# The first batch of a Mamba and expert layer: four transfers on each of two queues, and a wait for each block of u

## The chip, the cores and the metric

The kernel runs as one program on one core of a Trainium2 chip. The metric is the device time of one execution in microseconds (us); less is better. The core has a matrix engine (TensorE, PE in the rows; its weight loads are PEld), three engines for elementwise work (VectorE or DVE, ScalarE or ACT, GpSimd or POOL), and SyncE (SP), which here only issues DMA transfers. Each engine works through its own instructions in the order in which they are written, and waits on semaphores for the others.

## What is computed

Eight sequences of 512 tokens with 512 channels, all in float32. Each goes through a Mamba block, a residual with layer norm, a mixture of 8 experts (2 per token), and a second residual with layer norm. Cut to what matters here:

```python
xz = einsum('bld,ed->bel', hidden_states, in_proj_w)      # 512 -> 2 x 1024 channels
x, z = xz[:, :1024], xz[:, 1024:]
x = silu(causal_conv(x, conv_w, 4 taps) + conv_b)         # "u" in the kernel
x_dbl = einsum('bdl,kd->blk', x, x_proj_w)                # the x-projection: 1024 -> 64
dt_lo, B, C = x_dbl[..., :32], x_dbl[..., 32:48], x_dbl[..., 48:]
delta = softplus(dt_lo @ dt_proj_w.T + dt_proj_b)
h = h * exp(delta * A) + delta * B * x                    # 512 steps in time, 16 states
y = (sum(h * C) + x * D) * silu(z)
x1 = layernorm(hidden + y @ out_proj_w.T)
out = layernorm(x1 + top2_experts(x1))
```

## The kernel before, in words

The 1024 inner channels lie in 8 blocks of 128 partitions, the 512 tokens along the free dimension. The kernel is a pipeline over the batches. For each batch the three elementwise engines and TensorE run 128 rows (16 states by 8 channel blocks): ACT makes `dA` = exp(delta * A), POOL makes `dbu` = u * B, DVE runs the scan into `hst`, TensorE turns the result and DVE adds it into `y`. Between these rows a planner places, ahead of time, the pieces of the neighbouring batches: the projections of the next, the output and the experts of the one before. Its result is a fixed order of instructions on each engine.

The first batch has nothing to overlap with. Its pieces form a segment of their own, `SEG_FIRST`, which is run before any scan:

- `x`, j = 0..7: four matmuls (k = 0..3, named "shares") of `hT` (the batch's input, turned, four blocks of 128 x 512) with `W` (a 512-wide half of the input weights, `("Wx", 0)` in `delta[0][:, 0:4]` for j below 4, `("Wx", 1)` for the others) into one of two PSUM banks. In the trace each float32 matmul is two records, so one piece is 8 records. ACT then takes the first tap of the convolution (line 1247), DVE the other three (line 1528), and these free the bank.
- `sig`, `sig2`: the SiLU of each block, three ACT instructions and one product on POOL (line 1424), which raises `x_ready` by one for each block of `u`.
- `xproj`: eight shares, each a matmul of one block of `u` with `w_x`, summed in one bank (line 1035); ACT copies the sum to `xdbl`. Behind it stand `Ct` (line 1123) and, in turns, `yinit` (transposes of u * D, line 1067, copied by DVE) and `dt` (line 1129) with softplus on ACT (lines 1292 to 1299).
- POOL forms u = delta * u (line 1453) for each block, and then the first `dbu` (line 1465) and the first scan (line 1671) follow.

The loads of the head are issued by SP in the order written: `hT`, `("Wx", 0)`, the convolution's `cw` and `cb`, `("Wx", 1)`, `w_x`, nine small constants, the weights of z. `hidT_in` and `w_loaded[2]` tell PE that the first two have landed. The x-projection waits like this, and its waits stand ahead of its first share alone:

```python
if w.seg is SEG_FIRST:
    pe.wait_ge(const_in, 16 * NCONST)
    pe.wait_ge(pads_ready, 3)
pe.wait_ge(wx_in, w.p * 16 + 16)
pe.wait_ge(x_ready, w.p * ND + ND)
```

## Time and profile before

| | |
|---|---|
| median of 3 runs | 2383.67 us |
| lowest, highest | 2380.72, 2389.34 us |
| the profiled execution's own time | 2397.16 us |
| its span | 2395.4 us |
| PE busy | 2132.5 us (89% of the span) |
| DVE busy | 2120.6 us (89%) |
| POOL busy | 1804.7 us (75%) |
| ACT busy | 1517.4 us (63%) |
| span up to the first scan (DVE line 1671) | 84.1 us |

The first three lines are device times without the profiler. The others are of one profiled execution; its time is its span and 1.8 us around it. Busy shares are averages over the whole span: what one stretch waits for is read from its own rows.

### The profile page before, as it was taken

Reading aid. Unit: us, or ns where it says so; the run is one execution under the profiler, and the core shown is the slowest. Engines: PE = TensorE matmul, PEld = TensorE weight load, DVE = VectorE, ACT = ScalarE, POOL = GpSimd, SP = SyncE. Lnnn points to the kernel's source line nnn. Section 1 sums busy time; section 2 is a strip of 40 time slices with the busy share of each in tenths; the row PEclk is TensorE's granted clock in tenths of the full one; section 3 lists DMA queues with packets and bytes.
Section 4 is the critical chain, followed back from the end, with each engine's and each line's share of the span. In section 5 each row is a group of like instructions: output and inputs, shape, how many; then the busy total and the mean of one; then the engine's idle time right before and its main releaser. Section 6 shows DMA issues by size and latency. Waiting matters only on the chain. (4 is left out here: it accounts for less than half of the span.)

```text
span 2395.4 us, 30145 instructions
## 1 busy us (share of the span) xinstructions
PE 2132.5 (89%) x8604; PEld 1227.1 (51%) x8604; DVE 2120.6 (89%) x2440; ACT 1517.4 (63%) x2678; POOL 1804.7 (75%) x1448
## 2 busy tenths in 40 slices
PE   7886879898989989899899998899898998879998
PEld 2444555555545555545555555455555454555543
DVE  3799999999999899989999899998999898899933
ACT  3747755776577665668566675777657685565411
POOL 1759997788887888869887798878888697786502
PEclk9898789889998999989998899989999899879999
DMA  3312031347544584446752476445744467575523
GB/s 99 145 49 88 19 123 62 105 162 244 181 118 141 177 277 127 120 146 209 259 126 93 150 249 230 114 141 180 273 123 124 140 209 251 117 246 175 183 85 83
DMA packets 203683, 367.93 MB, mean 154 GB/s; under 512 B 28376, under 2 KB 32600, under 8 KB 203520
## 3 DMA queue, kind: packets, MB, share of 16 engines
q1 hardware_dynamic: 190976, 336.65, 42.3%
q0 software_dynamic: 12544, 29.37, 5.8%
q8 instruction: 71, 1.16, 0.2%
q14 instruction: 92, 0.75, 0.1%
HBM read 287.05 MB, written 78.91 MB: 153 GB/s over the span
## 5 line engine op out<-in xcount | busy, mean ns | idle before, releaser
L1465 POOL TENSOR_TENSOR dbu<-u,Bbc 128x512 f32<-128x512 f32 x896 | 1146.2, 1314 | 243.1 <-DVE hst L1671 234.9
L1671 DVE TENSOR_TENSOR_SCAN hst<-dA,dbu 128x512 f32<-128x512 f32 x896 | 1052.7, 1208 | 19.3 <-ACT dA L1370 15.0
L1370 ACT ACTIVATE dA<-delta,negA 128x512 f32<-128x512 f32 (+1 forms) x1152 | 724.4, 639 | 482.5 <-DVE hst L1671 388.8
L1049 PE MATMUL hTp<-ident,hst 128*128 128x128 f32 x4096 | 584.0, 295 | 126.6 <-DVE hst L1671 35.8
L1049 PEld LDWEIGHTS hTp<-ident,hst 128*128 128x128 f32 x4096 | 508.1, 152 | 363.5 <-issue 142.3
L1497 DVE SCALAR_TENSOR_TENSOR y<-hTp,Ct,y 128x1024 f32<-128x1024 f32 x512 | 647.4, 1265 | 46.6 <-PE hTp L1049 46.0
L1035 PE MATMUL bank<-wslot,hidT 128*128 128x512 f32 x512 | 238.9, 600 | 17.8 <-ACT zs L1314 13.8
L1035 PE MATMUL bank<-delta,tokT 128*128 128x512 f32 x480 | 224.4, 604 | 1.5 <-issue 0.8
L1035 PE MATMUL bank<-wslot,tokT 128*128 128x512 f32 x464 | 221.8, 608 | 2.7 <-ACT tokT L1329 1.7
L1473 POOL TENSOR_TENSOR dbu<-u,Bbc 128x512 f32<-128x512 f32 x128 | 163.3, 1311 | 80.0 <-DVE hst L1679 72.8
L1035 PE MATMUL bank<-hidT,wslot 128*128 128x512 f32 x384 | 193.6, 649 | 12.4 <-DVE u L1528 9.7
L1528 DVE SCALAR_TENSOR_TENSOR u<-bank,cw,u 128x511 f32<-128x511 f32 (+2 forms) x192 | 142.4, 744 | 35.9 <-ACT u L1247 31.1
L1035 PEld LDWEIGHTS bank<-wslot,hidT 128*128 128x128 f32 x512 | 91.9, 192 | 108.5 <-issue 85.8
L1418 POOL DMA_INDIRECT ysb<-sorted_results,place x52 | 81.4, 1566 | 85.9 <-DMA ysb<-x_scratch 76.6
L1035 PEld LDWEIGHTS bank<-wslot,tokT 128*128 128x128 f32 x464 | 83.3, 194 | 89.4 <-issue 80.0
L1035 PEld LDWEIGHTS bank<-delta,tokT 128*128 128x128 f32 x480 | 87.1, 195 | 81.3 <-issue 79.7
L1035 PEld LDWEIGHTS bank<-hidT,wslot 128*128 128x128 f32 x384 | 75.5, 209 | 101.7 <-issue 75.9
L1424 POOL TENSOR_TENSOR u<-u,side 128x512 f32<-128x512 f32 x64 | 81.6, 1275 | 57.0 <-ACT side L1265 56.8
L1453 POOL TENSOR_TENSOR u<-delta,u 128x512 f32<-128x512 f32 x64 | 81.9, 1280 | 28.9 <-DVE delta L1545 23.5
L1083 PE MATMUL hTp<-ident,zs 128*128 128x128 f32 x420 | 69.1, 309 | 29.2 <-DMA zs<-sorted_tokens 19.0
L1432 POOL TENSOR_TENSOR zs<-zs,side 128x512 f32<-128x512 f32 x64 | 87.7, 1370 | 9.9 <-ACT side L1321 9.9
L1247 ACT ACTIVATE u<-bank,cb,cw 128x512 f32<-128x512 f32 x64 | 49.5, 773 | 70.3 <-PE bank L1035 70.0
(149 smaller groups left out, 2558.9 us busy)
## 6 DMA issues: line engine op xcount, KB each, us to landing
wslot<-in_w_expT SPq DMA_DIRECT2D x85, 1024.0 KB, 6.3
Bbc<-b_scratch SPq DMA_DIRECT2D x113, 256.0 KB
zs<-sorted_tokens SPq DMA_DIRECT2D x105, 256.0 KB, 3.2
sorted_results<-ysb SPq DMA_DIRECT2D x105, 256.0 KB, 6.0
wslot<-in_w_inT SPq DMA_DIRECT2D x26, 1024.0 KB, 5.4
res<-in_w_expT SPq DMA_DIRECT2D x18, 1024.0 KB, 6.0
gate_scratch<-zs SPq DMA_DIRECT2D x64, 256.0 KB, 2.0
delta<-in_w_outT SPq DMA_DIRECT2D x14, 1024.0 KB, 9.8
```

What stands on the lines that cost most here:

```text
L1035: mm = nc.tensor.matmul(dst, lhs(k), rhs(k), start=(k == 0), stop=(k == n - 1))
L1049: mm = nc.tensor.transpose(hTp[q % 2][:, tok(j)], hst[n % 2][:, j, start:start + P], ident[:, :])
L1370: nc.scalar.activation(decay_of(step, halved), delta[w.odd][:, j, cols], ACT.Exp, scale=negA[:, j, n:n + 1]).then_inc(exp_done, 1)
L1418: nc.gpsimd.indirect_dma_start(rows_of(w, t), None, ys_dram[:, :], bass.IndirectOffsetOnAxis(ap=place[:, w.odd, t, c:c + 1], axis=0), comp ...
L1424: nc.gpsimd.tensor_tensor(x_j, x_j, side[j % 2][:, :], ALU.mult).then_inc(x_ready, 1)
L1432: nc.gpsimd.tensor_tensor(zs[i % 2][:, :], zs[i % 2][:, :], side[i % 2][:, :], ALU.mult).then_inc(z_ready, 1)
L1453: nc.gpsimd.tensor_tensor(x_j, d, x_j, ALU.mult).then_inc(u_ready, 1)
L1465: nc.gpsimd.tensor_tensor(dbu[j % 4][:, :], u[w.odd][:, j, :], Bbc[n % 2][:, :], ALU.mult).then_inc(dbu_done, 1)
L1473: nc.gpsimd.tensor_tensor(dbu[k % 4][:, :].rearrange("p (k t) -> p k t", k=2), u[w.odd][:, j:j + 2, cols], Bbc[n % 2][:, cols].unsqueeze(1 ...
L1497: nc.vector.scalar_tensor_tensor(y_part, hTp[q % 2][:, :], Ct[odd][:, t, n:n + 1], y_part, ALU.mult, ALU.add).then_inc(acc_done, 1)
L1528: tap = nc.vector.scalar_tensor_tensor(late, bank[s][:, 0:L - k], cw[:, j, TAPS - 1 - k:TAPS - k], late, ALU.mult, ALU.add)
L1671: nc.vector.tensor_tensor_scan(hst[n % 2][:, j, :], dA[j % 2][:, :], dbu[j % 4][:, :], 0.0, ALU.mult, ALU.add).then_inc(scan_done, 1)
```

## The change

The input `hT` of the first batch comes in four transfers, one for each block of 128 rows, each with a semaphore (`head_in`). Its first weights come in four transfers too, one for each 128 columns, that is for each of the pieces x 0 to x 3, each with a semaphore (`head_w`); they are issued by ACT ahead of its table load, on ACT's queue. A row of such a weight transfer has 128 floats (512 bytes) where it had 512 (2 KB). SP raises the two semaphores of before (`hidT_in`, `w_loaded[2]`) by hand, so that the counts of all later batches stay. The x-projection of the first batch waits for `x_ready` at each of its eight shares, for as many blocks of `u` as that share needs, and no more for all eight at its start.

```diff
@@ semaphores
+        head_in = [sem(f"head_in{k}") for k in range(KD)]
+        head_w = [sem(f"head_w{j}") for j in range(KD)]
@@ sync
-            sync.dma_start(hT[:, :, :], hidT[0].rearrange("(k p) t -> p k t", p=P)).then_inc(hidT_in, 16)
-            sync.dma_start(delta[0][:, 0:KD, :], block_src(("Wx", 0))).then_inc(w_loaded[2], 16)
+            for k in range(KD):
+                sync.dma_start(hT[:, k, :], hidT[0, k * P:(k + 1) * P, :]).then_inc(head_in[k], 16)
+            sync.sem_inc(hidT_in, 16)
+            sync.sem_inc(w_loaded[2], 16)
@@ tensor, piece "x"
                     if j == 0 and share == 0:
                         pe.wait_ge(hidT_in, w.p * 16 + 16)
+                    if w.seg is SEG_FIRST and share == 0 and j < KD:
+                        pe.wait_ge(head_w[j], 16)
+                    if w.seg is SEG_FIRST and j == 0:
+                        pe.wait_ge(head_in[share], 16)
@@ tensor, piece "xproj"
                         pe.wait_ge(wx_in, w.p * 16 + 16)
-                        pe.wait_ge(x_ready, w.p * ND + ND)
+                        if w.seg is not SEG_FIRST:
+                            pe.wait_ge(x_ready, w.p * ND + ND)
+                    if w.seg is SEG_FIRST:
+                        pe.wait_ge(x_ready, share + 1)
@@ scalar
+            for j in range(KD):
+                act.dma_start(delta[0][:, 0:KD, tok(j)], block_src(("Wx", 0))[:, :, tok(j)]).then_inc(head_w[j], 16)
             nc.scalar.preload_act_table_set("natural_log_exp_and_others")
```

On PE, at the start of the program and at the x-projection, the order before reads (a row is a line, an operation, output<-inputs and the waits in front of it; the last two rows of the first part are the x-projection and the transposes of `yinit`):

```order
L1035 MATMUL bank0<-hidT,delta0 128x512 [waits hidT_in,w_loaded2]
L1035 MATMUL bank0<-hidT,delta0 128x512 x3
L1035 MATMUL bank1<-hidT,delta0 128x512 [waits w_loaded2]
...
L1035 MATMUL bank0<-u0,spare0 64x512 [waits wx_in,pads_ready,x_ready,const_in,bank_taken0]
L1035 MATMUL bank0<-u0,spare0 64x512 x7
L1067 MATMUL hTp0<-ident,side0 128x128 [waits xd_ready]
```

and with the change:

```order
L1039 MATMUL bank0<-hidT,delta0 128x512 [waits head_w0,head_in0,hidT_in,w_loaded2]
L1039 MATMUL bank0<-hidT,delta0 128x512 [waits head_in1]
L1039 MATMUL bank0<-hidT,delta0 128x512 [waits head_in2]
L1039 MATMUL bank0<-hidT,delta0 128x512 [waits head_in3]
L1039 MATMUL bank1<-hidT,delta0 128x512 [waits head_w1,w_loaded2]
...
L1039 MATMUL bank0<-u0,spare0 64x512 [waits wx_in,pads_ready,x_ready,const_in,bank_taken0]
L1039 MATMUL bank0<-u0,spare0 64x512 [waits x_ready] x7
L1071 MATMUL hTp0<-ident,side0 128x128 [waits xd_ready]
```

No instruction of PE has moved: waits were added, and one wait is now spread over eight matmuls. At the start of ACT the order with the change is

```order
L1222 DMA delta<-in_w_inT 128x4x128 x4
L1223 ACT_TABLE_LOAD
L1260 ACTIVATE u<-bank,cb,cw 128x512 [waits bank_full0,conv_in]
```

so four issues of a DMA stand ahead of the table load, which was ACT's first instruction. On SP one transfer of 1 MB left its place as second, and the first became four.

## Rows read from the trace of the kernel before

**Rows 1.** The page: busy tenths of DVE in 40 equal slices.

```profile
DVE  3799999999999899989999899998999898899933
```

**Rows 2.** Waits of 0 to 60 us: engine, line <- releaser: total, times, longest.

```profile
PE bank L1035 <- DMA delta<-in_w_inT: 9.3, 1, 9.3
...
PE bank L1035 <- POOL u L1424: 7.0, 1, 7.0
```

**Rows 3.** Timeline of the head: start, us, engine, line, operation, [idle before].

```profile
0.75 0.44 SPq L783 DMA_DIRECT2D hidT<-in_hidT  x1
...
2.34 3.08 SPq L787 DMA_DIRECT2D cb<-in_conv_b  x1
5.46 3.22 SPq L788 DMA_DIRECT2D delta<-in_w_inT  x1
...
9.32 31.56 PE L1035 MATMUL bank<-hidT,delta 128*128 128x512 f32 x64 [9.32 <-DMA delta<-in_w_inT]
...
16.07 0.78 ACT L1247 ACTIVATE u<-bank,cb,cw 128x512 f32<-128x512 f32 x1 [14.05 <-PE bank L1035]
```

**Rows 4.** Busy time by stretch; the last three columns are clock, DMA share, GB/s.

```profile
0.00:2.00 2.00, 0.00 (x0) 0.00 (x0) 0.68 (x3) 1.25 (x1) 0.20 (x4) 1.00 0.08 8
2.00:4.00 2.00, 0.00 (x0) 0.00 (x0) 0.00 (x0) 0.03 (x1) 0.00 (x0) 1.00 0.94 216
4.00:5.00 1.00, 0.00 (x0) 0.00 (x0) 0.00 (x0) 0.00 (x0) 0.00 (x0) 1.00 1.06 414
5.00:6.00 1.00, 0.00 (x0) 0.00 (x0) 0.00 (x0) 0.00 (x0) 0.00 (x0) 1.00 1.04 399
6.00:8.00 2.00, 0.00 (x0) 0.00 (x0) 0.00 (x0) 0.00 (x0) 0.00 (x0) 1.00 1.04 395
...
13.00:14.00 1.00, 1.00 (x3) 0.48 (x2) 0.00 (x0) 0.00 (x0) 0.00 (x0) 1.00 1.27 272
...
26.00:28.00 2.00, 2.00 (x6) 0.91 (x5) 0.57 (x2) 1.70 (x3) 1.05 (x1) 1.00 0.00 0
```

**Rows 5.** DMA issues of 0 to 110 us: KB each, us from issue to landing.

```profile
hidT<-in_hidT SPq DMA_DIRECT2D x1, 1024.0 KB, 5.4
...
cb<-in_conv_b SPq DMA_DIRECT2D x1, 4.0 KB, 7.6
```

**Rows 6.** Timeline of TensorE's weight loads in the first piece.

```profile
14.60 0.34 PEld L1035 LDWEIGHTS bank<-hidT,delta 128*128 128x128 f32 x1 [0.52 <-issue]
...
15.81 0.19 PEld L1035 LDWEIGHTS bank<-hidT,delta 128*128 128x128 f32 x1 [0.24 <-issue]
```

**Rows 7.** Timeline of POOL: the last two of its eight products into u.

```profile
43.25 1.26 POOL L1424 TENSOR_TENSOR u<-u,side 128x512 f32<-128x512 f32 x1 [2.47 <-ACT side L1265]
46.47 1.26 POOL L1424 TENSOR_TENSOR u<-u,side 128x512 f32<-128x512 f32 x1 [1.95 <-ACT side L1265]
```

**Rows 8.** Timeline at the x-projection, and ACT's copy of it.

```profile
47.84 0.88 DVE L1536 TENSOR_SCALAR side<-u,dskip 128x512 f32<-128x512 f32 x2 [3.49 <-POOL u L1424]
...
47.88 9.52 PE L1035 MATMUL bank<-u,spare 128*64 128x512 f32 x16 [7.00 <-POOL u L1424]
...
57.43 0.59 ACT L1269 ACTIVATE rows<-bank 64x512 f32<-64x512 f32 x1 [10.84 <-PE bank L1035]
```

**Rows 9.** Busy time by stretch around the x-projection, columns as in rows 4.

```profile
48.00:52.00 4.00, 4.00 (x5) 1.04 (x6) 0.72 (x2) 0.00 (x0) 0.00 (x0) 0.50 0.00 0
...
53.00:56.00 3.00, 3.00 (x9) 0.95 (x8) 0.00 (x0) 0.00 (x0) 0.00 (x0) 1.00 0.00 0
```

**Rows 10.** Timeline from the x-projection to the first scan.

```profile
71.23 0.69 ACT L1292 ACTIVATE zs<-bank,dtb 128x512 f32<-128x512 f32 x1 [1.28 <-PE bank L1129]
...
82.76 9.86 POOL L1465 TENSOR_TENSOR dbu<-u,Bbc 128x512 f32<-128x512 f32 x8
84.13 6.12 DVE L1671 TENSOR_TENSOR_SCAN hst<-dA,dbu 128x512 f32<-128x512 f32 x5 [2.73 <-POOL dbu L1465]
```

**Rows 11.** Busy time by stretch after the first scan, columns as in rows 4.

```profile
84.00:400.00 316.00, 254.10 (x1032) 153.00 (x1031) 306.40 (x285) 214.52 (x354) 276.09 (x224) 0.86 0.21 71
```

## The prediction

> **What bounds the kernel now.** I read the page's slices first. DVE is at 8 or 9 tenths almost from end to end, but shows 3 and 7 in its first two slices of 60 us [rows 1]: there is a head that the pipeline doesn't fill. The stretch behind it does have a bound: from 84 to 400 us DVE is busy 306.4 of 316 us [rows 11]. So a head that is shorter by some us moves everything behind it forward by as much; nothing there waits for a fixed moment, since all its loads are issued in answer to this same work.
>
> In the head I looked at who waits for whom. TensorE has just two long waits in the first 60 us: 9.3 us for the transfer of the first weights, and 7.0 us for POOL's last product into u, ahead of the x-projection [rows 2]. Both lie on the chain to the first scan. From 9.32 us TensorE works through the x pieces with 31.56 us of work without a real gap [rows 3], so whatever starts it earlier moves the end of the x pieces, and POOL's products with them. And while the x-projection runs, ACT sits idle for 10.84 us until its copy at 57.43 [rows 8]. From there to the first `dbu` at 82.76 and the scan at 84.13 it is ACT's softplus that goes on, its longest pause behind the first `dt` 1.28 us [rows 10]. The change touches the two waits, and these alone.
>
> **The x-projection.** Its 16 records start at 47.88, when POOL's last product (46.47 + 1.26 = 47.73) is done, and end at 57.40 [rows 7, 8]. What will be left of it behind 47.88? By then TensorE has been free since 9.32 + 31.56 = 40.88 [rows 3]. The seventh block of u is ready at 43.25 + 1.26 = 44.51, the eighth 3.2 us later [rows 7]; the sixth, one such turn before the seventh, is ready at about 41, and the five before it are earlier. So shares 0 to 5 can run at once from about 41.0: 12 records. A record takes 0.43 us at TensorE's upper clock level (a weight load of 0.19 and 0.24 idle before it, at 15.81) and 0.86 us at the lower one (0.34 and 0.52, at 14.60) [rows 6]. They end at 41.0 + 12 x 0.43 = 46.2, share 6 at 47.0, and share 7 waits for POOL. Its two records start at 47.88 and 48.31, and the last takes some 0.6 us to its end (57.40 less 47.88 is 9.52; six starts 0.86 apart and nine 0.43 apart are 9.0 and leave the last record's own length of some 0.5 to 0.6): 48.9. The x-projection ends 57.4 - 48.9 = **8.5 us** earlier.
>
> This sum has a clock in it. In the trace the granted clock is 0.50 of full (the 1.2 GHz level) in the first 4 us of the x-projection and 1.00 (2.4 GHz) only from 53 us on [rows 9], after TensorE had stood still for 7.0 us [rows 2]. With the change it stands still for under 1 us in that place (47.0 to 47.88), so I take the upper level. Were share 7 alone at the lower level, it would end at 47.88 + 0.86 + 1.1 = 49.8 and the gain be 7.6; with all 16 records there, at 41.0 + 16 x 0.86 + 0.2 = 55.0, a gain of 2.4. [...]
>
> What stands behind: `yinit` needs DVE's two products, which start at 47.84 when the last block of u is there and take 0.88 us [rows 8], so they are ready at 48.7, before TensorE is. ACT has nothing else to do. Both waits that are passed at share 0 (`const_in`, `wx_in`) are for transfers of the head, and by 26 us nothing moves any more [rows 4]. The seven added waits sit on a queue that would idle anyway: nothing.
>
> **The head.** TensorE starts at 9.32 when 2 x 1.05 MB have landed. How fast do they come? From the GB/s of rows 4, times their length: 16 kB by 2 us, 448 kB by 4, 862 kB by 5, 1261 kB by 6, 2051 kB by 8. The 1.05 MB of `hT` are through at 5.5 by this count, and have landed for the semaphore at 0.75 + 5.4 = 6.15 [rows 3, 5], 0.7 us later. With the change the first matmul needs `hT`'s block 0 and the weights of x 0, 262 kB each. Rows of 512 bytes are nowhere near in the head as large transfers; the nearest are the 256-byte rows of `w_x`, at 272 GB/s around 13 us against 395 to 414 for 2 KB rows [rows 4]. So 262 kB of weights cost between 0.66 and 0.96 us; I add the whole 0.3 us.
>
> The unknown is how the 16 DMA engines share between two queues that are full at once; no stretch of the head shows it. Bounds: if they take turns by transfer, 524 kB come first, at 4.2 + 0.3 + 0.7 = 5.2 us. If ACT's queue with its small rows moves only as much as is left, the weights of x 0 come behind all of `hT`, after 1311 kB: 6.1 + 0.3 + 0.7 = 7.1 us. I take two blocks of `hT` ahead of them (786 kB, 4.8 + 0.3 + 0.7): **5.8 us, 3.5 us earlier**, with 4.1 and 2.2 as the bounds. The later blocks hide: x 0 runs at 1.7 us per share on the lower level (0.86 per record), so block 3 is wanted at 5.8 + 5.1 = 10.9 and x 1's weights at 12.6, while all 2.1 MB are through at about 8.2 + 1.2 + 0.7 = 10.1 (four weight transfers at 0.3 more each).
>
> ACT's first tap needs `cw` and `cb`. `cb` landed at 2.34 + 7.6 = 9.9 [rows 3, 5], and now stands behind half as much in its own queue, but shares the engines with rows that are up to 1.2 us slower: 11.1 at the latest. It is wanted when x 0 is done, 5.8 + 6.75 = 12.5 (ACT's tap came at 16.07, 6.75 us after TensorE's start) [rows 3]. The cover is 1.4 us. `("Wx", 1)`, whose issue sat for 3.22 us, is wanted at x 4, beyond 20 us. Four issues on ACT, at 0.44 us each as SP's first or at up to 3.2 each where they stall as SP's fifth did [rows 3], put the table load between 2.5 and 13.5 us, the last of which would just reach the 12.5; a stall at all four at once I don't expect. SP's two `sem_inc` come after four issues, at about 2.8 us: hidden.
>
> **The sum.** 8.5 + 3.5 = 12.0 us. The profiled execution took 2397.16 us and would take 2385.2; it lies 13.5 us above the median of the runs, and I take the same 12.0 off that: 2383.67 - 12.0 = **2371.7 us**, 0.50% less. What a measurement of this kernel can tell from no change is about 0.5%, here 11.9 us, so my forecast lies on that line.
>
> **The rivals.**
>
> *Weights behind all of hT.* TensorE starts at 7.1, the head gives 2.2: 10.7 in all, 2373.0 us. For it: 512-byte rows get little from turns taken row by row. Against: nothing in the trace.
>
> *The head gives nothing.* The first weights come only when all 2.1 MB are through, since the total to be moved is the same; then TensorE starts at 9.3 or later and 8.5 us are left: 2375.2 us. It would need ACT's queue to start after SP's is dry; ACT issues nothing before 0.74 us, as SP does, which speaks against it. The Trainium skill (DMA: Bandwidth & Descriptors, "Rules for kernel authors") speaks against this part of the change: it wants 1 MB and more in a transfer and says that a second issuing engine brings no bandwidth. By that rule the last byte comes no sooner, and this rival is what it gives if the first piece gets no turn of its own.
>
> *The x-projection stays slow.* TensorE's clock is at the lower level in the last shares, or in all: gain 7.6 or 2.4 in place of 8.5, with the head 11.1 or 5.9: 2372.6 to 2377.8 us.
>
> *What is behind the first scan gives or takes.* From 66 us TensorE was at the lower level and held ACT up for 1.28 us at 71.23 [rows 10]; which stretches are slow can fall otherwise. I allow 2 us either way: 2369.7 or 2373.7. A gain that is lost whole, at 2383.7, would need some work tied to the clock on the wall, and I see none.
>
> *Slower.* The waits at every share of x 0 keep TensorE from ever reaching the upper level in the x pieces. They have 64 records; at 0.86 us all take 55.0 in place of 31.56 us, 23.5 more. With 12.0 won that ends 11.5 later, 2395.2 us. It turns into a loss once some 28 more of the 64 records (12.0 / 0.43) run at the lower level than the first 7. The shares are wanted 1.7 us apart and come faster than that, so I give it little.
>
> **How the numbers follow.** Forecast (TensorE starts between 5.2 and 6.6, x-projection at the upper level): 0.52, and a little over a third of it falls short of the line by itself. Weights behind all of `hT`: 0.17. No gain from the head: 0.07. Slow x-projection: 0.08. More than 13 us: 0.08; some taken back behind: 0.05. Slower: 0.03. Faster by over 0.5% are some 0.32 of the forecast's 0.52, the 0.08, and what the scatter of the medians lifts over the line from the next ones, 0.06: 0.46. Slower by over 0.5%: 0.03. The rest, 0.51, is within. The range: the cases without a loss run from 2369.7 to 2377.8, and the three runs shown scatter by 3 to 6 us around their median, so 2365 to 2380.
>
> **What would show it.** In the profile of the changed kernel: TensorE's first matmul between 5.2 and 7.1 us, released by a DMA; records of the first piece at 0.86 us and no gap between its shares; ACT's first tap released by PE and not by `cb`; the x-projection split, most of it before POOL's last product, two records behind it, clock at 1.00; ACT's copy of it within 1.2 us of POOL's last product, where it was 9.7; the first scan near 72 us. It is wrong if the first scan comes at 72 and the end doesn't move with it, or if the first tap waits for its constants.

## The result, and the profile after

The changed kernel takes 2381.79 us (median of 20 runs, 2373.11 to 2388.38), the kernel before in the same measurement 2393.39 us (20 runs, 2377.06 to 2403.39). The ratio is 0.996 with a 95% interval of 0.9941 to 0.9978: by the ratio the change saves about 9.6 us, between 5.3 and 14.1 of 2393. (The two medians differ by 11.6 us, the two means by 9.7.) The forecast was 12.0 us less, a ratio of 0.995, and that is inside. The forecast time, 2371.7 us, and its range up to 2380 are both missed, because of the level that I took the 12.0 off: 2383.67 us from the three runs shown, where twenty say 2393.39.

The profiled execution took 2381.42 us, its span is 2379.6 (before: 2397.16 and 2395.4). The page's tenths of DVE, which answer to [rows 1], have 5 where they had 3 in the first slice; the second still has 7:

```profile
DVE  5799999999999999999999899998999898899833
```

The waits of 0 to 60 us, as in [rows 2]. Both long ones have shrunk, from 9.3 to 5.1 and from 7.0 to 0.8:

```profile
PE bank L1039 <- DMA delta<-in_w_inT: 5.1, 1, 5.1
...
PE bank L1039 <- POOL u L1437: 0.8, 1, 0.8
```

The timeline up to the copy of the x-projection, which answers to [rows 3, 7, 8]:

```profile
0.75 2.20 ACTq L1222 DMA_DIRECT2D delta<-in_w_inT  x4
0.76 1.81 SPq L786 DMA_DIRECT2D hidT<-in_hidT  x4
...
2.98 1.28 ACT L1223 ACT_TABLE_LOAD   x1 [2.98 <-issue]
3.25 1.04 SPq L791 DMA_DIRECT2D cb<-in_conv_b  x1
...
5.06 31.19 PE L1039 MATMUL bank<-hidT,delta 128*128 128x512 f32 x64 [5.06 <-DMA delta<-in_w_inT]
...
11.46 0.78 ACT L1260 ACTIVATE u<-bank,cb,cw 128x512 f32<-128x512 f32 x1 [7.20 <-PE bank L1039]
...
36.18 6.22 PE L1039 MATMUL bank<-u,spare 128*64 128x512 f32 x14
...
41.85 1.26 POOL L1437 TENSOR_TENSOR u<-u,side 128x512 f32<-128x512 f32 x1 [1.95 <-ACT side L1278]
43.16 1.07 PE L1039 MATMUL bank<-u,spare 128*64 128x512 f32 x2 [0.76 <-POOL u L1437]
44.27 0.59 ACT L1282 ACTIVATE rows<-bank 64x512 f32<-64x512 f32 x1 [2.30 <-PE bank L1039]
```

Read it in pairs with the rows of before. TensorE starts at 5.06 (9.32). The x pieces are 31.19 us of work (31.56). The x-projection is in two rows now: 14 of its 16 records run ahead of POOL's last product, which ends at 43.11, and two behind it, in 1.07 us. ACT's copy comes 1.16 us after that product, where it came 57.43 - 47.73 = 9.70 after it. So the copy is 57.43 - 44.27 = 13.16 us earlier: 4.26 by TensorE's start, 0.36 by the x pieces, and 9.70 - 1.16 = 8.54 by the x-projection.

The stretches of the head, columns as in [rows 4]:

```profile
2.00:4.00 2.00, 0.00 (x0) 0.00 (x0) 0.00 (x0) 1.02 (x1) 0.00 (x0) 1.00 0.90 278
4.00:5.00 1.00, 0.00 (x0) 0.00 (x0) 0.00 (x0) 0.26 (x1) 0.00 (x0) 1.00 1.09 367
...
6.00:8.00 2.00, 2.00 (x4) 0.92 (x3) 0.00 (x0) 0.00 (x0) 0.00 (x0) 1.00 1.12 324
```

The DMA issues of 0 to 98 us, columns as in [rows 5]:

```profile
hidT<-in_hidT SPq DMA_DIRECT2D x4, 256.0 KB, 4.9
...
cb<-in_conv_b SPq DMA_DIRECT2D x1, 4.0 KB, 7.4
```

And the timeline of TensorE's weight loads in the first piece, which answers to [rows 6]:

```profile
6.05 0.34 PEld L1039 LDWEIGHTS bank<-hidT,delta 128*128 128x128 f32 x1 [0.52 <-DMA hidT<-in_hidT]
...
10.77 0.19 PEld L1039 LDWEIGHTS bank<-hidT,delta 128*128 128x128 f32 x1 [0.24 <-issue]
```

In the last column of the stretches the transfers run at 324 to 367 GB/s where they ran at 395 to 414, and the traffic goes on beside TensorE instead of ahead of it. That the 512-byte rows cost something is borne out below, where 2 KB rows on both queues run at 404 to 405 GB/s from 5 to 8 us. Only the second block of `hT` is named as a releaser, and the 0.52 us ahead of it is the same as between any two records at the lower clock level: there is no gap in the first piece.

From the copy to the first scan it went less well. This is the timeline of the `dt` stretch up to the first scan:

```profile
56.14 0.69 ACT L1305 ACTIVATE zs<-bank,dtb 128x512 f32<-128x512 f32 x1 [1.45 <-PE bank L1140]
...
60.04 0.69 ACT L1305 ACTIVATE zs<-bank,dtb 128x512 f32<-128x512 f32 x1 [1.46 <-PE bank L1140]
...
72.94 6.12 DVE L1684 TENSOR_TENSOR_SCAN hst<-dA,dbu 128x512 f32<-128x512 f32 x5 [2.73 <-POOL dbu L1478]
```

And these are the stretches at its beginning, columns as in [rows 9]:

```profile
44.00:46.00 2.00, 2.00 (x17) 1.67 (x16) 1.02 (x3) 0.59 (x1) 0.00 (x0) 1.00 0.06 12
...
48.00:50.00 2.00, 2.00 (x9) 1.57 (x8) 0.49 (x1) 1.97 (x5) 0.00 (x0) 0.50 0.98 304
```

TensorE falls to the lower level (0.50) by 48 us, some 4 us behind the x-projection's end at 44.2; before it fell at about 66 us, 9 us behind the end at 57.4. ACT then waits twice for a `dt`, 1.45 and 1.46 us, where it waited once for 1.28 [rows 10]. From copy to first scan are 72.94 - 44.27 = 28.67 us, 1.97 more than the 26.70 of before. Of the 13.16 us at the copy, 84.13 - 72.94 = 11.19 are left at the first scan.

### The profile page after: what moved, and what is told of

It reads as the page before. It is cut to its first block, busy times and chain, and to the rows that moved or that the text cites. A ratio compares the mean times of both kernels' runs of the same rounds, so it can differ in the third digit from the quotient of the medians.

```text
span 2379.6 us, 30155 instructions
## 1 busy us (share of the span) xinstructions
PE 2125.3 (89%) x8604; PEld 1227.8 (52%) x8604; DVE 2117.5 (89%) x2440; ACT 1516.5 (64%) x2678; POOL 1802.8 (76%) x1448
## 3 DMA queue, kind: packets, MB, share of 16 engines
q8 instruction: 71, 1.16, 0.2%
## 4 chain that ended last, share of the span: by engine, by line
DVE 27%; PE 27%; POOL 23%; issue 12%; DMA 6%; ACT 4%; SPq 2%; DVEq 0%; POOLq 0%; ACTq 0%
PE bank L1039 17%; POOL dbu L1478 14%; DVE hst L1684 11%; DVE y L1510 7%; PE hTp L1053 5%; DVE u L1541 3%; DVE hst L1692 3%; POOL u L1466 3%; POOL delta L1463 2%; DMA zs<-sorted_tokens 2%; DMA ysb<-sorted_results,place 1%; PE bank L1172 1%; POOL dbu L1486 1%; DVE st L1516 1%; PE hTp L1087 1%
## 5 line engine op out<-in xcount | busy, mean ns | idle before, releaser
L1684 DVE TENSOR_TENSOR_SCAN hst<-dA,dbu 128x512 f32<-128x512 f32 x896 | 1051.7, 1205 | 18.5 <-ACT dA L1383 13.6
L1370 ACT ACTIVATE ysb<-bank 128x512 f32<-128x512 f32 x105 | 61.6, 587 | 48.3 <-PE bank L1039 38.0
## 6 DMA issues: line engine op xcount, KB each, us to landing
delta<-in_w_outT SPq DMA_DIRECT2D x14, 1024.0 KB, 10.4
```

What stands on the lines that cost most here:

```text
L1684: nc.vector.tensor_tensor_scan(hst[n % 2][:, j, :], dA[j % 2][:, :], dbu[j % 4][:, :], 0.0, ALU.mult, ALU.add).then_inc(scan_done, 1)
```

## The experiments

All times are in us. "Whole" is the ratio to the kernel before in the same measurement, with its 95% interval. Since the measurement can hardly tell 5 us, I also read from each profile when ACT copies the x-projection and when the first scan begins; before these are 57.43 and 84.13.

### One part of the change alone: the wait

The kernel before with the x-projection's wait split by share, and nothing else:

```diff
+                        if w.seg is not SEG_FIRST:
+                            pe.wait_ge(x_ready, w.p * ND + ND)
+                    if w.seg is SEG_FIRST:
+                        pe.wait_ge(x_ready, share + 1)
-                        pe.wait_ge(x_ready, w.p * ND + ND)
```

> The kernel before with the x-projection's wait split over its shares and nothing else. Theory (the two parts add, and a head that is shorter by x ends the kernel x earlier): TensorE starts at 9.3 as before, the x-projection's end and ACT's copy come 8.5 us earlier (copy at 48.9), the first scan 8.5 less some 2 us for TensorE's lower clock in the dt stretch, near 77.6; the time is 6 to 8.5 us less, ratio 0.997. Rival (the pipeline behind the first scan takes the gain back): the copy at 48.9 as well, but a ratio of 1.000.

Median of 12 runs 2386.95 beside 2389.48, whole 0.9982 (0.9963 to 1.0001), which just holds no gain at all. Its timeline:

```profile
9.36 30.19 PE L1035 MATMUL bank<-hidT,delta 128*128 128x512 f32 x64 [9.36 <-DMA delta<-in_w_inT]
...
46.46 1.07 PE L1035 MATMUL bank<-u,spare 128*64 128x512 f32 x2 [0.76 <-POOL u L1427]
...
47.57 0.60 ACT L1272 ACTIVATE rows<-bank 64x512 f32<-64x512 f32 x1 [2.31 <-PE bank L1035]
...
74.27 6.11 DVE L1674 TENSOR_TENSOR_SCAN hst<-dA,dbu 128x512 f32<-128x512 f32 x5 [2.73 <-POOL dbu L1468]
```

The copy is 9.86 us earlier. 1.37 of these are x pieces that take 30.19 in place of 31.56 us: three records fewer at the lower clock level (3 x 0.43), with the same instructions. The rest, 8.5, is the wait. From the copy to the first scan it is 26.70, exactly as before, although the wait is split: the 1.97 that the changed kernel's profile lost there do not come with the split.

### One part of the change alone: the head

The changed kernel with the single wait for all eight blocks put back:

```diff
-                        if w.seg is not SEG_FIRST:
-                            pe.wait_ge(x_ready, w.p * ND + ND)
-                    if w.seg is SEG_FIRST:
-                        pe.wait_ge(x_ready, share + 1)
+                        pe.wait_ge(x_ready, w.p * ND + ND)
```

> The changed kernel with the x-projection's single wait of before: only the transfers are split. Theory: TensorE starts at 5.1, POOL's last product comes 4.2 to 4.7 us earlier, the x-projection stands still for 7 us before it and takes 9.5 us as before, ACT's copy near 52.9, the first scan near 79.6; 4.5 us less, ratio 0.998. Rival (the gain of the two parts isn't a sum, since the earlier head also made the clock fall earlier in the dt stretch): first scan 2 us later than that, near 81.6, ratio 0.999.

Median of 12 runs 2389.17, whole 0.9994 (0.9976 to 1.0013). Its timeline:

```profile
4.99 8.57 PE L1039 MATMUL bank<-hidT,delta 128*128 128x512 f32 x16 [4.99 <-DMA delta<-in_w_inT]
...
42.57 8.50 PE L1039 MATMUL bank<-u,spare 128*64 128x512 f32 x16 [7.00 <-POOL u L1434]
...
78.90 6.11 DVE L1681 TENSOR_TENSOR_SCAN hst<-dA,dbu 128x512 f32<-128x512 f32 x5 [2.73 <-POOL dbu L1475]
```

TensorE starts 4.33 us earlier and the first scan comes 5.23 earlier. ACT's copy is at 51.11, 6.32 earlier: 4.33 by the start, 0.98 by the x pieces and 1.02 by an x-projection of 8.50 in place of 9.52 us. The stretch from the copy to the first scan is 27.79 and loses 1.09 of it. The interval of the whole, 3.1 us more to 5.7 less, holds a gain of 4.3 and also none. As the ratios stand, the two parts save 4.3 and 1.4, 5.7 us together, where the change saves 9.6; the intervals are too wide to tell whether they add. The last section of the experiments takes more out of the same runs.

### Which part of the x-projection's 9.5 us is the clock

The wait stays whole, but TensorE works through its pause: seven matmuls of unused data into a buffer that nothing reads yet. The output doesn't change.

```diff
+            def filler(n, cols=512):
+                for _ in range(n):
+                    nc.tensor.matmul(dA[0][:, 0:cols], ident[:, :], wslot[0][:, 0, 0:cols], start=True, stop=True)
@@ tensor, piece "xproj"
+                        if w.seg is SEG_FIRST:
+                            pe.wait_ge(w_loaded[0], 16)
+                            filler(7)
                         pe.wait_ge(wx_in, w.p * 16 + 16)
                         pe.wait_ge(x_ready, w.p * ND + ND)
```

> The kernel before with seven matmuls that nobody reads (identity by z weights, into a PSUM tile that is still unused) between the last x piece and the x-projection, where TensorE stands still for 7.0 us. The wait isn't split. Theory (2.4 us of the 8.5 are the clock, 6 the shares that were run ahead): the granted clock stays at 1.00, the x-projection takes 7.0 in place of 9.5 us, ACT's copy near 54.9; ratio 0.999. Rival (the clock isn't lowered by the pause): the x-projection still takes 9.5 us and the copy stays at 57.4.

Median of 12 runs 2388.95, whole 0.999 (0.9967 to 1.0012). Its timeline:

```profile
39.50 6.23 PE L1041 MATMUL dA<-wslot,ident 128*128 128x512 f32 x14
...
46.67 7.05 PE L1035 MATMUL bank<-u,spare 128*64 128x512 f32 x16 [0.94 <-POOL u L1432]
...
53.76 0.59 ACT L1277 ACTIVATE rows<-bank 64x512 f32<-64x512 f32 x1 [8.38 <-PE bank L1035]
...
82.69 2.45 DVE L1679 TENSOR_TENSOR_SCAN hst<-dA,dbu 128x512 f32<-128x512 f32 x2 [2.73 <-POOL dbu L1473]
```

The same 16 records take 7.05 us, and 9.52 where TensorE had stood still. So of the 8.5 us that the wait was worth, 2.5 are the clock that the pause had cost, and 6.0 are 14 records that run ahead of the last product: 14 x 0.43. What the same pause of 7.0 us costs differs from profile to profile: the 16 records behind it took 8.50 us with the head alone, 8.98 with late `yinit` alone, 9.22 with the 56 records more and 9.52 in the kernel before, which is 1.5 to 2.5 us above the 7.05. The Trainium skill (TensorE: Matmul & The Clock Gate, "Why this matters for your kernels") says that an idle gap between bursts of matmuls brings the clock down; these profiles agree. It is not only a gap that does: in the `dt` stretch above, the clock was at 0.50 with TensorE counted busy for 2.00 of 2.00 us.

The copy comes 3.67 us earlier, the first scan only 1.44. From the copy to the scan are 28.93 us here, 2.23 more than in the kernel before, and nothing of the change is in this kernel: the changed kernel's loss in this stretch also comes without the change.

### Does a shift of the head reach the end

A gain that is lost on the way would be lost as a delay, too. The first piece is computed seven more times before it is used, 56 records; the output doesn't change.

```diff
+                    if w.seg is SEG_FIRST and j == 0 and share == 0:
+                        for _ in range(7):
+                            accumulate(ps[:, :], lambda k: W[:, k, tok(j % KD)], lambda k: hT[:, k, :], KD)
```

> The kernel before with the first x piece computed eight times over instead of once (28 more matmuls of 0.86 us, 24.1 us), the last of which is used. It lengthens the head by a known amount, larger than the scatter of the runs. Theory (the head passes to the end one for one): the first scan near 108.2 and the time 24 us more, ratio 1.010. Rival (the pipeline behind has slack that gives or takes some): a ratio of 1.007 or less; the same share would then be missing of the change's own gain, 8 of 11.2 us.

```profile
9.27 55.13 PE L1035 MATMUL bank<-hidT,delta 128*128 128x512 f32 x120 [9.27 <-DMA delta<-in_w_inT]
...
107.35 6.11 DVE L1674 TENSOR_TENSOR_SCAN hst<-dA,dbu 128x512 f32<-128x512 f32 x5 [2.72 <-POOL dbu L1468]
```

The first scan is 23.22 us later, and the median of 6 runs is 2417.16, whole 1.0106 (1.008 to 1.0132), which is 25.3 us with an interval of 19.1 to 31.5. What the head costs, the end costs, within that interval: the rival, a ratio of 1.007 or less, is ruled out, a loss or gain of a few us on the way is not.

### Does the lost time come from the transposes of yinit, or from the clock

In the `dt` stretch TensorE does the transposes of `yinit` between the matmuls of `dt`. First, the last two of these `yinit` pieces go behind the last `dt`:

```diff
+def at_end(rows, late):
+    rows[:] = [x for x in rows if x not in late] + [x for x in rows if x in late]
+at_end(SEG_FIRST.rows["pe"][0], [(("yinit", j), 0) for j in (6, 7)])
+at_end(SEG_FIRST.rows["dve"][0], [("yinit", j) for j in (6, 7)])
```

> The changed kernel with the last two transposes of yinit (j = 6, 7) behind the last dt on TensorE, and their copies at the end of the segment on DVE. It tests what the stretch from ACT's copy of the x-projection to the first scan is made of: 26.70 us before, 28.67 us with the change. Theory (TensorE at the lower clock takes 1.97 us for a pair of yinit and 2.07 for a dt, more than the 2.3 to 2.6 us per block that ACT's softplus needs, so ACT pauses twice for 1.45 us): one of the two pauses goes and the stretch is near 27.3 us, or 26.7 if the clock stays up longer this time. Rival (DVE's copies and the transfers that run beside it, not TensorE, hold the stretch): it stays at 28.7.

One execution: 2369.14 beside 2389.86 for the kernel before. Its timeline:

```profile
43.39 0.59 ACT L1289 ACTIVATE rows<-bank 64x512 f32<-64x512 f32 x1 [2.30 <-PE bank L1046]
46.46 0.69 ACT L1312 ACTIVATE zs<-bank,dtb 128x512 f32<-128x512 f32 x1 [2.48 <-PE bank L1147]
...
68.69 6.11 DVE L1691 TENSOR_TENSOR_SCAN hst<-dA,dbu 128x512 f32<-128x512 f32 x5 [1.53 <-POOL dbu L1485]
```

From copy to scan 25.30 us and no pause of ACT behind its first `dt`, less than the 26.7 to 27.3 that I expected. But the clock stayed up longer too: it fell 9.0 us behind the copy, in the changed kernel's profile 3.6. So this profile alone doesn't tell the order from the clock; the table further down does. Second, the order stays, and half a full-size matmul of unused data runs ahead of each `dt`, to keep TensorE busy (output unchanged):

```diff
                     if w.seg is SEG_FIRST:
+                        if j == 0:
+                            pe.wait_ge(w_loaded[0], 16)
+                        filler(1, 256)
                     mm = nc.tensor.matmul(ps[:, :], w_dt[:, j * P:(j + 1) * P], xdbl[0:RANK, :], start=True, stop=True)
```

> The changed kernel with half a matmul of filler (identity by z weights, 256 columns, 0.43 us at the upper clock level, read by nobody) ahead of each dt. Theory (it is the clock that lengthens the stretch): the granted clock stays at 1.00 longer than to 47.9 us and ACT's pauses of 1.45 us shrink or go; the stretch from ACT's copy to the first scan is 26.7 to 27.5 us. Rival (fillers are only more work in TensorE's queue): the clock falls all the same and the stretch is over 29 us.

One execution: 2385.22. The stretches from its copy (44.19) on:

```profile
44.00:50.00 6.00, 6.00 (x30) 3.54 (x30) 2.49 (x7) 2.67 (x5) 0.00 (x0) 1.00 0.39 130
50.00:60.00 10.00, 9.14 (x39) 4.49 (x37) 8.87 (x14) 9.04 (x16) 3.99 (x3) 1.00 1.03 356
```

The clock is at 1.00 where it had been 0.50 from 48 us on (it falls at 64.6), and only one of ACT's pauses stands, 0.86 us. But each `dt` now waits for its filler (the first came 0.63 us later), and the scan starts 26.93 after the copy, 0.23 more than in the kernel before and 1.74 less than in the changed kernel's profile. So the clock alone, with the order as it was, takes most of the loss away, and the filler has a cost of its own.

### Two queues or one, columns or rows

The same eight transfers, all on SP's queue, `hT` and weights in turns:

```diff
             for k in range(KD):
                 sync.dma_start(hT[:, k, :], hidT[0, k * P:(k + 1) * P, :]).then_inc(head_in[k], 16)
+                sync.dma_start(delta[0][:, 0:KD, tok(k)], block_src(("Wx", 0))[:, :, tok(k)]).then_inc(head_w[k], 16)
-            for j in range(KD):
-                act.dma_start(delta[0][:, 0:KD, tok(j)], block_src(("Wx", 0))[:, :, tok(j)]).then_inc(head_w[j], 16)
```

> The changed kernel with the four weight transfers on SP's queue as well, in turns with those of the input. Theory (what counts is that the first 0.5 MB hold all that the first matmul needs, not which queue they are on): TensorE starts at 5.1 as with two queues, within 0.4. Rival (two queues are what gets the weights there early): TensorE starts at 5.8 or later, since the weights are issued one by one behind the input's blocks.

One execution: 2380.07. Its timeline:

```profile
4.86 9.25 PE L1040 MATMUL bank<-hidT,delta 128*128 128x512 f32 x16 [4.86 <-SPq L789]
...
11.25 0.78 ACT L1259 ACTIVATE u<-bank,cb,cw 128x512 f32<-128x512 f32 x1 [9.22 <-DMA cb<-in_conv_b]
```

The timeline of TensorE's weight loads in its first piece:

```profile
8.00 0.29 PEld L1040 LDWEIGHTS bank<-hidT,delta 128*128 128x128 f32 x1 [0.93 <-DMA hidT<-in_hidT]
...
9.55 0.30 PEld L1040 LDWEIGHTS bank<-hidT,delta 128*128 128x128 f32 x2 [0.78 <-DMA hidT<-in_hidT]
```

One queue starts TensorE 0.2 us earlier still (4.86 here and in the last kernel below, 4.99 to 5.21 in six profiles with two queues). Then the weights of x 1 to x 3 stand ahead of the `hT` blocks of x 0, and its shares wait for them (0.93, 0.78). Copy at 44.06, first scan at 70.76: no worse than two queues. For the start of TensorE the second queue brings nothing. What brings the start forward is that the first piece waits for less. Of bandwidth, the Trainium skill (DMA: Bandwidth & Descriptors, "Rules for kernel authors") says that more issuing engines don't help, since all transfers share the same DMA engines. From 6 to 8 us these profiles agree (357 GB/s with one queue, 324 with two); but by 8 us, summed over the stretches, the one queue had moved some 1.7 MB and the two 1.9, since the one queue dropped to 108 GB/s between 4 and 5 us. Why it did is open.

Second, the weights on ACT's queue again, cut by their 128 rows k in place of columns, so that each row of a transfer keeps its 2 KB and share k of x 0 waits for block k:

```diff
+            for k in range(KD):
+                act.dma_start(delta[0][:, k, :], block_src(("Wx", 0))[:, k, :]).then_inc(head_w[k], 16)
@@ tensor, piece "x", j == 0
+                        pe.wait_ge(head_w[share], 16)
                         pe.wait_ge(head_in[share], 16)
```

> The changed kernel with the first weights cut by their 128 rows, each 512 wide (2 KB rows), in place of by 128 columns (512-byte rows): share k of x 0 waits for input block k and weight block k, the later pieces for nothing. Theory (small rows cost up to 0.3 us per 262 kB): TensorE starts near 4.9, and the first 2.1 MB are through about 1 us earlier; the first scan no more than 0.3 us from that of the changed kernel but for the clock. Rival (the last weight block, wanted by share 3 of x 0, comes too late): a gap of over 0.5 us in the first piece.

One execution: 2389.40. Its timeline:

```profile
5.62 31.22 PE L1039 MATMUL bank<-hidT,delta 128*128 128x512 f32 x64 [5.62 <-DMA delta<-in_w_inT]
```

Its DMA issues of 0 to 110 us:

```profile
hidT<-in_hidT SPq DMA_DIRECT2D x4, 256.0 KB, 5.7
```

And a stretch of its head, columns as in [rows 4]:

```profile
4.00:5.00 1.00, 0.00 (x0) 0.00 (x0) 0.00 (x0) 0.00 (x0) 0.00 (x0) 1.00 0.77 275
```

TensorE starts 0.56 us later than with the 512-byte rows, where I had expected 4.9. The blocks of `hT` take 5.7 us to land where the changed kernel's took 4.9. The larger rows didn't take a larger share for the weights: less was moved in all. By 5 us it is some 0.67 MB, with a DMA share of 0.77 from 4 to 5 us, and in the changed kernel 0.95 MB, with 1.09. From 5 to 8 us the 2 KB rows run at 404 to 405 GB/s, faster than the 512-byte rows (324 to 343), too late for the first matmul. It is one execution, and why the two queues begin more slowly with 2 KB rows is open.

### The change again, and combinations

The changed kernel once more, as it is, in the same measurement as the three below:

> The changed kernel once more, to set it beside the variants on one chip. Theory (what comes off the head comes off the end): the head in its profile is 10.5 to 13.5 us shorter than before (first scan at 70.7 to 73.6, by how early TensorE's clock falls in the dt stretch), and the ratio is 0.9945 to 0.9975. Rival (part of it is given back behind the first scan): 0.9975 or more, although the first scan is as early as in the first run.

Median of 12 runs 2383.08 beside 2391.90 (34 runs of the kernel before), whole 0.996 (0.9943 to 0.9977): the same number, in a second measurement. In its profile the copy is at 43.91 and the first scan at 70.63, 26.72 apart. This is the changed kernel without the 1.97 us of loss: the same instructions give both. One line is new:

```profile
11.07 0.78 ACT L1260 ACTIVATE u<-bank,cb,cw 128x512 f32<-128x512 f32 x1 [6.71 <-DMA cb<-in_conv_b]
```

ACT's first tap waited for `cb`. Behind that tap TensorE had a gap of 0.20 us ahead of its third piece.

The changed kernel with the two late `yinit` pieces (the edit above):

> The changed kernel with the last two transposes of yinit behind the last dt, timed. In one look ACT had no pause among its softplus blocks, and the stretch from its copy of the x-projection to the first scan took 25.3 us against 26.7 to 28.9 in the other kernels. Theory: 1.4 to 3.4 us better than the changed kernel; ratio to the kernel before 0.994. Rival (the look was lucky and the clock decides): the same ratio as the changed kernel within 0.001.

Median of 12 runs 2376.49, whole 0.9944 (0.9923 to 0.9966), the lowest of all. Its interval and that of the change overlap from 0.9943 to 0.9966. Set against each other, the 12 runs of this kernel have a mean 5.1 us below the 12 of the change again, with a 95% interval of some 0.8 to 9.4; but their mean clock is higher too (0.918 against 0.9155), and at equal clock 1.2 +- 2.7 are left. So it is not clearly shown to be better than the change. In its profile:

```profile
44.52 0.59 ACT L1289 ACTIVATE rows<-bank 64x512 f32<-64x512 f32 x1 [2.31 <-PE bank L1046]
...
56.28 0.69 ACT L1312 ACTIVATE zs<-bank,dtb 128x512 f32<-128x512 f32 x1 [1.45 <-PE bank L1147]
...
71.54 3.68 DVE L1691 TENSOR_TENSOR_SCAN hst<-dA,dbu 128x512 f32<-128x512 f32 x3 [1.53 <-POOL dbu L1485]
```

27.02 from copy to scan: with one pause of ACT, and still 1.65 less than the changed kernel with its two.

The late `yinit` pieces in the kernel before:

> The kernel before with the last two transposes of yinit behind the last dt, and nothing of the change. Theory (the order in the dt stretch is worth something by itself, and independent of the change): ACT's copy at 57.4 as before or up to 1.4 us earlier by the clock, the stretch from there to the first scan 25.3 us in place of 26.7, ratio 0.9993. Rival: the stretch stays at 26.7, since before the change the clock fell so late in it that TensorE held ACT up only once.

Median of 12 runs 2395.77, whole 1.0017 (0.9998 to 1.0036). In its profile the copy is at 55.69 and the first scan at 80.99, 25.30 apart: 1.4 us are won up to there and none of it is seen in the time of the whole.

All of it: the change with eight transfers in one queue and the late `yinit`:

> The changed kernel with both: the weight transfers on SP's queue in turns with the input's, and the late yinit transposes. With one queue TensorE started at 4.86 against 5.06. Theory (the parts add): first scan near 68.5, ratio 0.994, the best of all. Rival (cw and cb, which now stand behind eight transfers on one queue, hold ACT's first tap up): the tap comes later than 6.5 us after TensorE's start, with ACT waiting for a DMA.

Median of 11 runs 2381.59, whole 0.9966 (0.9945 to 0.9986). In its profile the copy is at 44.35 and the first scan at 69.65, 25.30 apart, the earliest scan but for the first late `yinit` profile (68.69), and yet no gain over the change, where I had expected the best of all. `cb` held the first tap up here as well:

```profile
11.53 0.78 ACT L1266 ACTIVATE u<-bank,cb,cw 128x512 f32<-128x512 f32 x1 [9.51 <-DMA cb<-in_conv_b]
```

With these profiles, order and clock in the stretch from copy to scan can be told apart. The time at which the clock falls is read from stretches of 1 us:

| kernels | clock falls, behind the copy | copy to first scan |
|---|---|---|
| old order: before, wait alone, 56 records more, one queue, the change again | 8.8 to 9.5 | 26.69 to 26.72 |
| old order: head alone | 4.6 | 27.79 |
| old order: the change, pause filled, row blocks | 3.4 to 3.7 | 28.64 to 28.93 |
| late `yinit`: the first profile, in the kernel before, all in one queue | 8.5 to 9.2 | 25.30 |
| late `yinit`: the change and late `yinit` | 3.7 | 27.02 |
| old order with filler ahead of each `dt` | 20.4 | 26.93 |

At the same order an early fall costs 1.7 to 2.2 us; at the same time of the fall the late transposes save 1.4 to 1.9. These are two effects, and neither is the change's: the early fall is there without the change (pause filled), and the late one with it (the change again).

### What else the same runs tell: time against granted clock

Each run lists TensorE's mean granted clock beside its time. Over the 64 runs of the kernel before in these measurements the clock lies between 0.912 and 0.922. The ten runs at 0.920 have a median of 2385.0 us, the ten at 0.916 one of 2394.1; time and clock are correlated by -0.76 (-0.80 over the 20 runs of the changed kernel). One common slope through all runs, with a constant of its own for each kernel, is -1365 us per 1.0 of clock, or 13.6 us per 0.01, and what is left scatters by 3.3 us. At equal clock the kernels differ from the one before by:

| kernel | at equal clock, 95% | first scan in the profile |
|---|---|---|
| wait alone | -7.4 +- 2.1 | -9.9 |
| head alone | -3.0 +- 2.1 | -5.2 |
| the change, 20 runs | -9.0 +- 1.7 | -11.2 |
| the change again | -9.4 +- 2.1 | -13.5 |
| pause filled | -2.4 +- 2.0 | -1.4 |
| 56 records more | +25.1 +- 2.8 | +23.2 |
| change and late `yinit` | -10.6 +- 2.1 | -12.6 |
| late `yinit` alone | +1.6 +- 2.1 | -3.1 |
| all, in one queue | -9.7 +- 2.1 | -14.5 |

The two parts add: 7.4 + 3.0 = 10.4, against 9.0 and 9.4 for both. This reads the clock as luck of the run. It would hide a gain that comes as a higher clock, and no run sets the clock, so it is only a second reading of the same data.

The right column is 1.9 to 4.8 us lower than the left one, even for the 56 records, but for the filled pause, where it is 1.0 higher. Part of that is the profile of before itself: its x pieces took 31.56 us, those of three other kernels with the old head 30.19, 30.23 and 30.48. With a typical 30.2 its first scan would stand at about 82.8, and each number on the right be 1.3 higher. What is left for the change again (-12.2 against -9.4), the late `yinit` (-1.8 against +1.6) and the last row (-13.2 against -9.7) isn't explained.

Where the clock comes in can be seen in the batches. I cut the trace between the first indirect transfers of POOL in two successive batches, where the same 1070 records of TensorE lie. One such stretch of the kernel before, columns as in [rows 4]:

```profile
932.00:1211.70 279.70, 257.53 (x1070) 149.57 (x1069) 258.51 (x282) 189.94 (x325) 230.09 (x184) 0.93 0.54 173
```

The same stretch of the changed kernel:

```profile
919.70:1192.80 273.10, 247.94 (x1070) 144.11 (x1069) 257.51 (x282) 189.48 (x325) 229.81 (x184) 0.96 0.56 177
```

Up to here the changed kernel was 932.0 - 919.7 = 12.3 us ahead, the head's gain and little else. In this one batch it gains 6.6 more, with DVE, ACT and POOL as busy as before and TensorE at 0.96 in place of 0.93, and in later ones it loses some: at the end it is 15.8 ahead. The 14 profiles have 56 such stretches (four each): they take from 273.2 us, at a clock of 0.96, to 283.0, at 0.92, with DVE busy 257.3 to 258.8 in every one. The scatter of a whole run adds up from such steps. That the clock is what makes them is the natural reading and not shown, since nothing here sets it.

## Why the prediction was right, and where it was wrong

**The level: wrong, and it decided.** The step that failed is "13.5 us above the median of the runs, and I take the same 12.0 off that: 2383.67 - 12.0", with "the three runs shown scatter by 3 to 6 us around their median" as the range's allowance. Three runs of a kernel that spreads over 26 us (2377.06 to 2403.39) say little of its median, and the three lay low: the median of the twenty, which hold the three, is 9.7 us above theirs, and in the later 64 runs only about one in ten is at 2383.67 or below. The profiled execution's 2397.16 had told it: it was no overhead of the profiler, as the changed kernel's 2381.42 beside a median of 2381.79 shows, but an ordinary run at clock 0.915. Taken off 2393.39, the same 12.0 give 2381.4; that this is within 0.4 of the 2381.79 is in part luck, since the gain by the ratio is 9.6. The range also breaks its own rule: 3 to 6 us of scatter on top of the 2377.8 would have ended it at 2381 to 2384, and I let it end at 2380, 2.2 above.

**The x-projection, 8.5: right.** Alone and in the change 8.5 us in the profile. Shares 0 to 6 ran ahead of POOL's last product, two records behind it, at the upper level. Its working had two halves, records that run ahead and the clock's return; the filled pause measures them as 6.0 and 2.5. The 2.5 hold for the profile before; by other profiles the pause costs from 1.5.

**The head, 3.5: right in kind, a little small.** The term was mis-sized by the start: 5.8 forecast, 5.06 measured, below even the bound of 5.2 (4.99 to 5.21 in five other profiles with the same transfers). I had put two blocks of `hT` ahead of the first weights, and the two queues took turns better than that: 4.3 us. In the sum of the time it is 3.0 +- 2.1 at equal clock. The weights behind all of `hT` (7.1) and no gain from the head (9.3) are both ruled out by the start at 5.06.

**The cover of the first tap, 1.4 us: about used up.** In the profiled run the tap was released by PE, as forecast, and so it was in three other profiles of kernels with the split head; in five it was released by `cb`. The longest wait of TensorE that this left behind was 0.47 us ahead of the third piece (in the kernel with the head alone), 0.20 in the change's second profile. So "wrong if the first tap waits for its constants" came true at a price of next to nothing. The forecast had `cb` by 11.1 at the latest, and it landed at 3.25 + 7.4 = 10.65; what used the cover up is the tap, wanted at 11.46 and not at 12.5, since TensorE started 0.7 us earlier than forecast and had fewer records at the lower level.

**The stretch behind the x-projection, +-2 us: right, nearly to its end.** The profiled run lost 1.97 in the `dt` stretch since TensorE's clock fell 4 us behind the x-projection and not 9. The same instructions lost nothing in the second profile of the change, and the kernel before with its pause filled lost 2.23 without the change. So the loss lies in where the fall comes (the table above); that the change itself moves the fall is not shown by any run, nor is what does. Fewer transposes ahead of the `dt` make the stretch less open to it.

**The slower rival: didn't happen.** The first piece had no gap; the x pieces took 30.2 to 31.6 us in all the profiles (but for the one that computes 56 records more).

**Does it reach the end: yes, within what can be told.** The added 23.2 us of head came to 25.3 (19.1 to 31.5) at the end, and the 11 us of the profile to 9.6 (5.3 to 14.1). One to two microseconds less at the end than at the first scan remain possible and open.

## What to carry to other kernels

Where a first stage has nothing to overlap with, let each consumer wait for just the part that it reads: the gain can be worked out to half a microsecond from the last producer's end and the number of consumer steps left behind it, and here it reached the end, within an interval of some 4 us each way, behind a steady part that is bound. A pause that goes takes its slow clock with it, so count the steps at the level that they will have. And take the level of a forecast from many runs, or forecast the difference alone: three runs and a median, with a profiled time 13.5 us above that median, were the sign that the scatter is larger than the gain.

## What the runs showed of the hardware that I had not expected

- The scatter of this kernel from run to run, +-13 us or +-0.5%, goes with TensorE's mean granted clock (0.912 to 0.922 in 64 runs of the kernel before, correlation -0.76), at some 13.6 us per 0.01. A batch of the same 1070 records took 273.2 us at 0.96 and 283.0 at 0.92.
- After the same instructions the clock falls at different times: 3.6 us behind ACT's copy in one profile of the changed kernel, 9.5 in another, and that alone moves the first scan by 1.95 us. In the stretch of transposes and 32-row matmuls TensorE is counted busy all the time (2.00 of 2.00 us) and still goes to 0.50; half a full-size matmul ahead of each `dt` held it at 1.00 until 64 us.
- Two queues that are full at once gave both first transfers (262 kB each) by 5.06 us, one queue in turns by 4.86; with 2 KB rows on the second queue in place of 512-byte rows it was 5.62, one execution, with fewer bytes moved by then.
- A 4 KB transfer (`cb`) issued behind 1 MB on its queue, with another 1 MB on a second queue, landed 7.1 to 7.8 us after its issue in seven profiles, and after 7.6 with all 2 MB ahead of it on one queue: half of its queue gone brought it almost nothing. Behind eight transfers on one queue it was issued later, at 5.5 to 6.0 us, and landed after 5.8 and 5.5.
